# Weight loads of a mixture-of-experts kernel: both kinds of load alternate between two issuing queues

## The reference

```python
gate_logits = jnp.einsum('bsd,ed->bse', x, Wg)
top_v, top_i = jax.lax.top_k(gate_logits, TOP_K)
...
gating = jax.nn.softmax(sparse_logits, axis=-1)
h1 = jnp.einsum('bsd,ehd->bseh', x, W1)
h2 = jnp.einsum('bsd,ehd->bseh', x, W2)
hidden = jax.nn.silu(h1) * h2
expert_out = jnp.einsum('bseh,edh->bsed', hidden, W3)
return jnp.einsum('bsed,bse->bsd', expert_out, gating)
```

## Time and profile before

| | us |
|---|---|
| median of 2 timed runs | 6896.1 (6877.8 to 6914.4) |
| the profiled execution | 6876.0 |
| its span on the slowest core, core 0 | 6874.4 |
| spans of the other cores | 6817.1 to 6849.8 |
| PE busy with matmuls | 4928.8 |
| first matmul of the first pass | at 2141.8 |
| last matmul of the last pass ends | at 6736.3 |

### The profile page before, as it was taken

How to read it: one execution, slowest core, us unless ns; L and a number is a source line. 1 busy time by engine, 2 the same in 40 slices (tenths; PEclk the granted TensorE clock), 3 DMA queues, 4 the chain that set the end, 5 groups by cost and what they waited for, 6 DMA issues and landing times.

```text
span 6874.4 us, 59536 instructions; the slowest of 8 cores (6817.1 to 6874.4 us)
## 1 busy us (share of the span) xinstructions
PE 4928.8 (72%) x20119; PEld 1997.2 (29%) x20519; DVE 1370.6 (20%) x2544; ACT 860.3 (13%) x1235; POOL 622.1 (9%) x1152
## 2 busy tenths in 40 slices
PE   6667787700146888888888788888878887888881
PEld 2222222200012333333333333333333333333330
DVE  3552111000153111111111111111111111111114
ACT  0003555400001000100011000010001100001100
POOL 1000111111000100001000010000100000100000
PEclk8766777755577999999999999999999999999996
DMA  6235999999703444444344444444444434444431
GB/s 106 47 66 119 203 198 205 205 206 209 165 34 86 119 121 122 129 121 120 114 128 125 118 118 117 120 128 123 118 114 124 128 112 122 119 114 129 120 113 67
DMA packets 928048, 868.18 MB, mean 126 GB/s; under 512 B 62976, under 2 KB 786176, under 8 KB 927504
## 3 DMA queue, kind: packets, MB, share of 16 engines
q1 hardware_dynamic: 790448, 528.55, 25.5%
q0 software_dynamic: 137312, 335.79, 23.8%
HBM read 866.32 MB, written 146.80 MB: 147 GB/s over the span
## 4 chain that ended last, share of the span: by engine, by line
PE 54%; DMA 31%; issue 7%; DVE 6%; ACT 1%; DVEq 0%; another core or an unknown queue 0%; POOL 0%; POOLq 0%; SPq 0%; ACTq 0%
PE pS L889 38%; PE px L889 16%; DMA w3s<-w3b 14%; DMA w12b<-wtb 5%; DMA wtb<-w12i 4%; DMA wtb<-w3p 3%; DMA w3b<-wtb 3%; DVE rbuf L889 1%; DVE cbuf L889 1%; DVE oac L889 1%; DVE lnm L889 1%; DMA wstage<-wq 1%; DMA out<-outb 1%; DVE V L889 0%; DVE gBt L889 0%
## 5 line engine op out<-in xcount | busy, mean ns | idle before, releaser
L889 PE MATMUL pS<-uA,w12s 128*128 128x512 bf16 x5517 | 1332.2, 382 | 69.3 <-DVE x1te L889 40.7
L889 PE MATMUL pS<-w3s,hiddenG 128*128 128x512 bf16 x2759 | 748.5, 392 | 682.1 <-DMA w3s<-w3b 626.2
L889 ACT ACTIVATE s1b<-pS 128x512 bf16<-128x512 f32 x704 | 420.5, 597 | 4108.6 <-PE pS L889 4003.8
L889 PEld LDWEIGHTS pS<-uA,w12s 128*128 128x128 bf16 x5632 | 551.4, 98 | 740.7 <-issue 89.4
L889 POOL DMA_DIRECT2D w3s<-w3b x704 | 379.3, 539 | 4198.6 <-PE px L889 4061.0
L889 PE MATMUL px<-w3s,hiddenG 128*128 128x512 bf16 x2761 | 745.9, 392 | 3.2 <-issue 0.4
L889 PE MATMUL pS<-x1te,w12s 128*128 128x512 bf16 x3012 | 725.9, 381 | 3.3
L889 PE MATMUL px<-x1te,w12s 128*128 128x512 bf16 x2508 | 600.0, 379 | 2.6
L889 PEld LDWEIGHTS pS<-w3s,hiddenG 128*128 128x128 bf16 x2816 | 239.5, 99 | 1158.2 <-issue 990.0
L889 DVE TENSOR_TENSOR hiddenG<-s1b,pS 128x512 bf16<-128x512 bf16 x384 | 263.7, 687 | 1018.6 <-PE pS L889 999.2
L889 DVE TENSOR_TENSOR oac<-pS,oac 128x512 f32<-128x512 f32 x128 | 79.4, 682 | 1923.6 <-PE px L889 1923.6
(11 more groups left out here) (100 smaller groups left out, 2053.5 us busy)
## 6 DMA issues: line engine op xcount, KB each, us to landing
w12s<-w12b SPq DMA_DIRECT2D x704, 512.0 KB, 4.0
w3s<-w3b POOLq DMA_DIRECT2D x704, 256.0 KB, 2.9
wtb<-w12i POOLq DMA_DIRECT2D x234, 384.0 KB, 8.0
w12b<-wtb SPq DMA_DIRECT2D x234, 384.0 KB, 6.1
wtb<-w3p POOLq DMA_DIRECT2D x117, 384.0 KB, 8.0
w3b<-wtb SPq DMA_DIRECT2D x117, 384.0 KB, 6.4
xres<-x SPq DMA_DIRECT2D x16, 512.0 KB, 3.5
out<-outb SPq DMA_DIRECT2D x16, 512.0 KB, 2.6
```

The costliest lines, as they stand in the source:

```text
L889: inst = getattr(engine, meth)(*a, **k)
```

## The change

`w12_load` and `w3_load` choose the engine that waits for the buffer and issues the DMA by the buffer's number: W12 slices with an even number stay with SP and those with an odd number go to POOL; W3 slices with an even number stay with POOL and those with an odd number go to SP. Buffers, sizes, semaphores and the places in the code at which the loads are written stay. The `gRow` load stays with POOL.

```diff
     def w12_load(e, ts, ht):
         buf = ht % 4
-        S.slot_wait("sync", ("w12s", buf))
+        q = "sync" if buf % 2 == 0 else "gpsimd"
+        S.slot_wait(q, ("w12s", buf))
...
-        m_w12[(e, ts, ht)] = S.dma("sync", dstb, srcb, f"rl{buf}")
+        m_w12[(e, ts, ht)] = S.dma(q, dstb, srcb, f"rl{buf}")
 
     def w3_load(e, ts, ht):
         buf = ht % 2
-        S.slot_wait("gpsimd", ("w3s", buf))
+        q = "gpsimd" if buf == 0 else "sync"
+        S.slot_wait(q, ("w3s", buf))
         m_w3[(e, ts, ht)] = S.dma(
-            "gpsimd", w3s[:, buf, :],
+            q, w3s[:, buf, :],
```

## The result

The changed kernel takes 1.0346 times as long as the kernel before, with a 95% interval of 1.0304 to 1.0389 (some executions, of both kernels, are disturbed and are left out of every ratio here). Its profiled execution took 7100.3 us against 6876.0: 224 us more, where 98 were forecast. The direction was right; the size lies beyond the range, whose upper end, 7070, is a ratio of 1.028.

A forecast was written before the change was run, and what follows sets the result against it. The prediction took the output stage to be bound by its two W3 buffer loops. Boundary waits with half clock (+197 us) less the output stage's gain (-99) gave +98 on 6876.0: 6974 us, range 6885 to 7070.

The forecast's parts named there:

- What bounds the output stage: Output stage: PE waits for W3 loads because each of two buffers has its own loop, not for bandwidth; 626 us.
- The two loops of 5.5 us: W3 buffers: matmuls to request 2.4, landing 2.9, PE 0.2; odd loop falls to about 5.1, even stays, gain nothing.
- The rival of late W3 loads on SP: Output stage: SP's W3 loads landing at 4.0 us make the odd loop 6.2, 224 us more, 7198; chance 0.06.
- The place of the new wait: Between passes: W12 slice 0 stands behind W3 slice 1 on SP, so the first `pS<-uA,w12s` matmul idles 6 to 7 us.
- No bandwidth, no effect: Whole kernel: several issuing engines save only sequencer time, so 6876 us; chance 0.13 together with a cheap wait.
- The price of the new wait: At 24 plain boundaries: PE starts at E + 6.8 instead of E + 0.94, 5.9 us each, bounds 3.9 and 7.1.
- The upper bound, E + 7.8: Boundary between passes: latest landing of W12 slice 0, five loads served in turn, 7.0 us plus 2.0 fixed from E - 1.2.
- The clock: First matmuls after the boundary idle run at half clock, costing 2.3 us at each of 24 boundaries.
- The changes of expert: At 7 boundaries PE already starts about 9 us after E, for `x1te`; the W12 load lands inside that, no cost.
- What the output stage gives back: Output stage: four early W12 loads leave its start, 3.2 us shorter in 31 passes, -99 us; bounds 1.0 and 4.6.
- My control: Last pass, with no next W12 loads: output stage 58.0 us against 61.2 in pass 6, used to size the gain.
- The boundary wait at its full price: Between passes: POOL's backlog served first and longer half clock, 242 us lost, 71 regained, 7047 us; chance 0.20.

The follow-up runs named there:

- The run that holds POOL back: The changed kernel, with POOL requesting W12 slices 1 and 3 only after the last W3 matmul of the pass before; ratio 1.0166 to the kernel before.
- the run with two bursts: Only odd W3 slices moved to SP, plus three unused 512 KB SP loads behind W12 slices 6 and 13 each pass; mean output stage 61.41 us, against 60.59.

## Why the prediction came out as it did

**What bounds the output stage: right.** The two loops of 5.5 us, of which the slower sets the pace, explain why one odd loop made faster gained nothing. The landing of a W3 load on SP, bounded from 2.7 to 4.0 and taken as 2.9, is 3.0; the first packet comes 1.2 us behind the issue on both queues (medians in the output stages, 1.17 on SP and 1.24 on POOL). The rival of late W3 loads on SP falls with it. That four buffers bring the stage to 38 us confirms the reading.

**The place of the new wait: right.** It stands ahead of `pS<-uA,w12s`, is ended by a W12 load, and goes away when the loads are written ahead of the output stage (0.9983). So "No bandwidth, no effect" is right in its first half, as the Trainium skill has it ("DMA: Bandwidth & Descriptors", Issuing engines are not separate DMA queues), and wrong in its second: the queues bring nothing, but their order costs 3.5%.

**The price of the new wait: mis-sized, and this is the step that failed.** The step was "POOL's W3 slice 0 and W12 slices 1 and 3 are just under way ... 3.3 x 1.3 / 2.1 = 2.0 late, so E + 6.6". With POOL's two W12 loads absent, PE started at E + 5.9; with them, at E + 9.8. They cost 3.9 us, twice the 2.0 that I scaled for everything that slice 0 meets; in all slice 0 landed at E + 9.4, 4.8 us later than alone. The upper bound, E + 7.8, was no bound: it let five loads be served one after the other and left out the sixth, W12 slice 2, which stands behind slice 0 in SP's own queue, and it took 0.30 MB per us where 0.27 were carried in the 8 us behind E of pass 6 (268 GB/s in 3186.43 to 3194.43). The landings of the loads behind pass 6 of core 1, by narrow stretches of the DMA view (us from issue to landing), in the order of the requests at 3185.38 (POOL, slice 1), 3186.91 (SP, slice 0) and then those of SP under way in 3187.2 to 3187.4 (slices 0 and 2, so that the median is the middle of the two):

```profile
w12s<-w12b POOLq DMA_DIRECT2D x1, 512.0 KB, 7.1
```

```profile
w12s<-w12b SPq DMA_DIRECT2D x1, 512.0 KB, 9.3
```

```profile
w12s<-w12b SPq DMA_DIRECT2D x2, 512.0 KB, 9.9
```

Slice 0 lands at 3186.91 + 9.3 = 3196.2. As 9.9 is the middle of 9.3 and slice 2's own time, slice 2 took 10.5 from 3187.4 and landed at 3197.9, 1.7 us later. The queues of the one microsecond from 3192 to 3193 show who was served (packets, MB, share of 16 engines):

```profile
q0 software_dynamic: 60, 0.25, 84.9%
q1 hardware_dynamic: 104, 0.05, 22.9%
```

POOL's 60 packets carry 0.25 MB and SP's 104 carry 0.05. I took this for the cause, engines that take turns by packet with POOL's packets larger, as the Trainium skill says of their turns ("DMA: Bandwidth & Descriptors", Queues, rings and completion order). The run that holds POOL back measured against it: with the same packets in both queues, POOL's asked for 0.25 and 1.3 us behind slice 0, slice 0 came 3.6 us sooner. What the queues had carried when slice 0 landed tells what the lead is worth (packets, MB, share). First the changed kernel, from the request of W3 slice 0 to the landing, 3184.73 to 3196.20; then the same stretch with POOL held back, core 2 behind pass 10, 3782.45 to 3789.33:

```profile
q1 hardware_dynamic: 2165, 1.28, 42.8%
q0 software_dynamic: 368, 1.31, 42.0%
```

```profile
q1 hardware_dynamic: 1571, 0.98, 51.2%
q0 software_dynamic: 99, 0.34, 14.9%
```

In the changed kernel all of POOL's 1.3 MB went before slice 0 was there, and of SP's 1.28 MB only 0.79 are W3 slice 1 and slice 0: the rest, 0.5 MB, is slice 2's. With POOL held back its queue carried 0.34 MB by then, of which 0.26 are W3 slice 0. Over all plain boundaries POOL's queue carried 1.27 MB before slice 0's last packet in the one case and 0.33 in the other (SP's bytes counted off in the order of its requests). The difference, 0.94 MB at 0.27 MB per us, is 3.5 us, an estimate that meets the 3.6 measured. So asking sooner let the whole of POOL's 1 MB be carried first. Whether the order of the requests alone does that, or the unequal turns have a part in it, is not shown.

**The clock: right.** +51 us against +55. The half clock stands in the stretch 3189.50 to 3199.70 of the changed kernel (us, busy times, granted clock, DMA share, GB/s), over the end of the idle and the first matmuls:

```profile
3189.50:3199.70 10.20, 3.15 (x8) 1.20 (x9) 1.90 (x4) 0.00 (x0) 0.00 (x0) 0.50 0.68 184
```

Over all 32 passes it costs 1.6 us each, whether the idle was 5.9 or 9.7 us, since the hidden stage is 78.2 in all these runs. The passes behind a change of expert had it before as well (78.2 us); at the 24 plain boundaries the stage grew from 76.1 to 78.2, 2.1 us each against the 2.3 that I took.

**The changes of expert: a bound was too near.** I put PE's start at about 9 us after E and called the load hidden. On core 1 it landed at E + 9.8 in the mean, later than `x1te` was made, and PE started at E + 10.1: +8 us.

**What the output stage gives back: the mechanism right, the control wrong.** This is the second term that was mis-sized, -41 us for -99. The delay by the early W12 loads did go. In pass 6 of core 1 slices 0 and 2 start 5.46 us apart (3125.49 and 3130.95) where it was 6.45, with no half clock behind:

```profile
3125.49 1.02 PE L891 MATMUL pS<-w3s,hiddenG 128*128 128x512 bf16 x4 [1.50 <-DVE gBt L891]
...
3130.95 1.02 PE L891 MATMUL pS<-w3s,hiddenG 128*128 128x512 bf16 x4 [1.85 <-DMA w3s<-w3b]
```

On core 0 the mean stage fell from 62.53 to 59.66, by 2.9 us, close to my 3.2. But core 1, which sets the time, fell only to 61.22 (its own mean was 62.17 before). In 29 of its 31 first output stages one W3 load is late: PE is idle for 2.6 us or more in place of 1.8, and in 22 of the 29 its matmuls then start 0.427 us apart in place of 0.216, which is half clock. Core 0 has no such idle at all. The timelines of both cores in pass 5 and in pass 29, core 1 first and core 0 behind it:

```profile
3014.19 1.02 PE L891 MATMUL pS<-w3s,hiddenG 128*128 128x512 bf16 x4 [3.66 <-DMA w3s<-w3b]
...
6607.36 1.86 PE L891 MATMUL pS<-w3s,hiddenG 128*128 128x512 bf16 x4 [3.19 <-DMA w3s<-w3b]
```

```profile
3018.45 3.29 PE L891 MATMUL pS<-uA,w12s 128*128 128x512 bf16 x8 [10.17 <-DMA w12s<-w12b]
...
6609.67 2.72 PE L891 MATMUL pS<-uA,w12s 128*128 128x512 bf16 x6 [9.80 <-DMA w12s<-w12b]
```

Core 0's pass 5 ends at 3018.45 - 10.17 = 3008.3 and core 1's long idle begins at 3014.19 - 3.66 = 3010.5, 2.2 us later by their two clocks; in pass 29 it is 6599.9 and 6604.2, 4.3 us. Over all 29 the distance stays between 1.3 and 6.7 us, while the place of the idle within core 1's own stage moves from 53.7 us after its start (pass 0) to 3.6 (pass 21, and from there on). So the late load goes with core 0's boundary, the moment when core 0 asks for its six loads at once, and not with a fixed place in core 1's stage. The same holds for cores 2 and 3, 5 and 4, 7 and 6: with one fixed distance for each pair, 89 to 100% of the idles of over 2.5 us fall within 2.5 us of the neighbour's boundary. In each pair one core is hit and the other isn't, which is also why the spans of the changed kernel fall in two groups, 7032 to 7037 and 7093 to 7099 us. My control, the last pass, had no early loads of its own, but no neighbour at a boundary either, for core 1's last output stage is 57.74 us and that of core 0, whose neighbour is still at work, 61.16. That the neighbour's burst is the cause, and not only at the same time, is shown by the run with two bursts, where new bursts brought new late loads at the same distance; what in the chip the two cores share is not shown.

**Rivals.** "The boundary wait at its full price" was the one that came: 20% was given to it and 7047 us, where the execution took 7100. It named the same place and too low a bound. What the prediction held against it, that POOL's requests lead SP's by only 1 to 2 us, was true and no objection: leads of 1.0 us and of nothing were enough. (The upper end of the range, 7087 less a tenth of the width, would be 7065 and not 7070; that changes nothing.)

## What to carry to other kernels

When loads are dealt out to several queues, write down each queue's list across the end of a stage: a prefetch that lands behind a load which waits for the stage's last instruction is no prefetch, and here that cost 3.5%, all of it undone by moving four loads up in the same lists. A stage that waits for its loads is a loop of landing plus use of a buffer, and more buffers (626 us of waiting down to 7), not more queues, shorten it. A bound for a late transfer must hold everything that the core has asked for by then, the loads behind it in its own queue too, and a pass taken as control must have neighbours that do what they do elsewhere.

## What the runs showed of the hardware

- 1 MB in the other queue, its first half asked for 1.0 us ahead of a load and its second half at the same time, holds the load back by 3.9 us (idle 9.7 against 5.9 without it); the same 1 MB asked for 0.25 and 1.3 us behind the load costs it 0.2 (6.1 against 5.9).
- Cores 0 and 1, 2 and 3, 4 and 5, 6 and 7 disturb each other: a burst of 2.6 MB on one (the six loads of a boundary) makes a W3 load on the other land some 1.5 us late, and an added burst of 1.6 MB (three loads of 512 KB) does so too.
- A W12 load of the same shape is about 1024 packets on SP's queue. q0 carried 137 thousand packets before and 160 thousand with 352 of them added and 352 W3 loads of some 80 packets each taken away, so on POOL's queue it is about 144, an estimate from these counts; the median landing is alike (4.6 us on SP, 4.8 on POOL).
- The same kernel's mean output stage differed by 1.0 us from one chip to the next (59.55 and 60.59), more than one of the effects (0.8 us) that I tried to measure from one chip to another.
